# A one-hot product in four row strips, and a new order of the first splits

## What is computed

```
W   = weights[condition]                      # weights: 16 x 32 x 32, condition: 32 numbers in 0..15
mix = einsum('bct,bcd->bdt', x, W)            # every sequence b mixed by its own 32 x 32 matrix
q, k, v = mix @ Wq + bq, mix @ Wk + bk, mix @ Wv + bv        # 512 -> 4096, 32 heads of 128
```

## Time and profile before

| | us |
|---|---|
| median of 3 runs | 806.32 |
| lowest and highest of them | 806.26 and 807.01 |
| the profiled execution's own time | 805.49 |
| its span, first to last instruction | 803.7 |

### The profile page before, as it was taken

How to read it: one execution, slowest core, us unless ns; L and a number is a source line. 1 busy time by engine, 2 the same in 40 slices (tenths; PEclk the granted TensorE clock), 3 DMA queues, 4 the chain that set the end, 5 groups by cost and what they waited for, 6 DMA issues and landing times.

```text
span 803.7 us, 15196 instructions
## 1 busy us (share of the span) xinstructions
PE 795.6 (99%) x6093; PEld 651.7 (81%) x6093; DVE 643.1 (80%) x646; ACT 332.2 (41%) x374; POOL 520.5 (65%) x451
## 2 busy tenths in 40 slices
PE   9999999999999999999999999999999999999998
PEld 7777888888888888888888888888888888888466
DVE  7799888888888888987889769989899888861442
ACT  4655555555555555572222226322422331322520
POOL 4999887333333333428998995979999999910420
PEclk9999999999999999999999999999999999999999
DMA  7031111111111111304434421456404813418502
GB/s 207 28 85 50 52 52 52 53 52 52 52 52 52 52 52 42 115 2 157 182 139 180 180 105 55 169 79 187 157 1 157 316 61 147 157 50 257 127 18 88
DMA packets 80735, 81.87 MB, mean 102 GB/s; under 512 B 26044, under 2 KB 61212, under 8 KB 78652
## 3 DMA queue, kind: packets, MB, share of 16 engines
q1 hardware_dynamic: 80188, 81.24, 31.2%
q10 hardware_dynamic: 512, 0.13, 0.1%
HBM read 64.97 MB, written 16.40 MB: 101 GB/s over the span
## 4 chain that ended last, share of the span: by engine, by line
PE 91%; DVE 3%; POOL 3%; ACT 2%; DMA 1%; issue 1%; SPq 0%; DVEq 0%; POOLq 0%
PE psum L862 13%; PE psum L864 12%; PE psum L863 12%; PE psum L808 7%; PE psum L810 7%; PE psum L809 7%; PE psum L1061 7%; PE psum L1090 4%; PE psum L1092 4%; PE psum L1091 4%; PE psum L1078 3%; PE psum L1080 3%; PE psum L1079 3%; PE psum L901 3%; PE psum L1149 1%; DMA w_raw<-in_wk 1%
## 5 line engine op out<-in xcount | busy, mean ns | idle before, releaser
L506 POOL TENSOR_TENSOR w_raw<-w_raw 128x256 f32<-128x256 f32 x31 | 45.1, 1454 | 123.1 <-DMA w_raw<-in_wk 122.6
L862 PE MATMUL psum<-t_hi,w_hi 128*128 128x512 f32 x248 | 100.5, 405 | 0.0
L864 PE MATMUL psum<-t_hi,w_lo 128*128 128x512 f32 x248 | 96.5, 389 | 0.0
L863 PE MATMUL psum<-t_lo,w_hi 128*128 128x512 f32 x248 | 96.5, 389 | 0.0
L1370 ACT ACTIVATE sq<-qk_sb 128x1024 f32<-128x1024 f32 x31 | 32.9, 1063 | 140.7 <-issue 127.5
L1637 DVE TENSOR_TENSOR sumsq<-sumsq,sq 128x1024 f32<-128x1024 f32 x62 | 80.2, 1295 | 0.0
L1409 ACT ACTIVATE at_hi<-psum,params 128x512 fp32r<-128x512 f32 x64 | 44.0, 688 | 69.6 <-PE psum L1061 69.6
L862 PE MATMUL psum<-mix_hi,w_hi 128*128 128x512 f32 x186 | 72.5, 390 | 0.2 <-DVE w_lo L1541 0.2
L863 PE MATMUL psum<-mix_lo,w_hi 128*128 128x512 f32 x186 | 72.4, 389 | 0.0
L864 PE MATMUL psum<-mix_hi,w_lo 128*128 128x512 f32 x186 | 72.4, 389 | 0.0
L1541 DVE TENSOR_TENSOR w_lo<-w_raw,w_hi 128x1792 fp32r<-128x1792 f32 x30 | 61.4, 2047 | 1.5 <-ACT w_hi L1246 1.5
(11 more groups left out here) (287 smaller groups left out, 2130.2 us busy)
## 6 DMA issues: line engine op xcount, KB each, us to landing
v_sb<-v_scr_dram SPq DMA_DIRECT2D x6, 2048.0 KB, 7.9
v_scr_dram<-v_sb SPq DMA_DIRECT2D x9, 1024.0 KB, 3.9
w_raw<-in_wq SPq DMA_DIRECT2D x32, 256.0 KB, 2.9
w_raw<-in_wk SPq DMA_DIRECT2D x32, 256.0 KB, 3.2
wv_raw<-in_wv SPq DMA_DIRECT2D x16, 512.0 KB, 4.4
toep<-kpad_dram SPq DMA_DIRECT2D x2, 4096.0 KB, 14.5
wo_raw_a<-in_wo SPq DMA_DIRECT2D x4, 1024.0 KB, 5.2
wo_raw_b<-in_wo SPq DMA_DIRECT2D x4, 1024.0 KB, 5.2
```

The costliest lines, as they stand in the source:

```text
L862: mm(bank(n), wh, hi[:, c, tok], start=(i == 0), stop=False)
L863: mm(bank(n), wh, lo[:, c, tok], start=False, stop=False)
L864: last = mm(bank(n), wl, hi[:, c, tok], start=False, stop=(i == 1))
```

## The change

The product that chooses W is cut in four strips. `cond_nat` holds at partitions 0, 32, 64 and 96 the 16 rows of 256 numbers that belong to one quarter of the columns; two of these loads are issued by SyncE, two by ScalarE's queue behind `cond_i`, which now goes to all 128 partitions. Each strip is one matmul of 256 columns over 16 partitions at its own row position of the array, into a bank of its own (0 to 3). One semaphore count behind the last one replaces the two of before. The blanking of `cond_nat` goes; three small operations subtract 32, 64 and 96 from the partition numbers instead. Both turns into `mix_w` read all four banks. TensorE spins six times ahead of the product and eight times behind it. On ScalarE and VectorE the split of head 0's weights moves behind two groups, and VectorE writes the `mix_f` of group 4 one group later.

```diff
-            for n in range(2):
-                sp.dma_start(cond_nat[NCOND * n:NCOND * n + NCOND], cond_w.rearrange("n c d -> n (c d)")).then_inc(cond_in, 16)
+            for i in range(2):
+                sp.dma_start(cond_nat[32 * i:32 * i + NCOND], cond_cols[i]).then_inc(cond_in, 16)
...
-            spin(5, ones[:, :], 7)
-            pe.wait_ge(cond_in, 48)
+            spin(6, ones[:, :], 7)
+            pe.wait_ge(cond_in, 80)
             pe.wait_ge(hot_ok, 1)
-            pe.wait_ge(fill_ok, 2)
-            for n in range(2):
-                mm(bank(n), onehot[:].rearrange("n q b -> n (q b)"),
-                   cond_nat[:].rearrange("n (c d) -> n c d", d=32)[:, :, 16 * n:16 * n + 16],
-                   start=True, stop=True).then_inc(mixw_mm, 1)
-            spin(3, ones[:, :], 7)
+            for i in range(4):
+                rows = slice(32 * i, 32 * i + NCOND)
+                last = mm(bank(i, 256), onehot[rows].rearrange("n q b -> n (q b)"), cond_nat[rows, :],
+                          start=True, stop=True, tile_position=(32 * i, 0))
+            last.then_inc(mixw_mm, 1)
+            spin(8, ones[:, :], 7)
...
-            act.dma_start(cond_i[:], every_partition(cond_idx, BATCH, NCOND)).then_inc(cond_in, 16)
+            act.dma_start(cond_i[:], every_partition(cond_idx, BATCH)).then_inc(cond_in, 16)
+            for i in range(2, 4):
+                act.dma_start(cond_nat[32 * i:32 * i + NCOND], cond_cols[i]).then_inc(cond_in, 16)
...
+            for n in range(2):
+                mix_out(n)
             act.wait_ge(w_in[0], 32)
             sc.activation(w_hi[0][:, 0:4, :].rearrange("p b n -> p (b n)"),
                           w_raw[0][:, 0:4, :].rearrange("p b n -> p (b n)"), ACT.Copy).then_inc(whi0_ok, 1)
-            for n in range(G):
+            for n in range(2, G):
                 mix_out(n)
...
             v.memset(cond_f[:], -1.0).then_inc(zero_ok, 1)
-            v.memset(cond_nat[64:P], 0.0).then_inc(fill_ok, 1)
-            v.memset(cond_nat[32:64], 0.0).then_inc(fill_ok, 1)
+            dve.wait_ge(sel_const, 1)
+            for q in range(1, 4):
+                v.tensor_scalar(cond_no[quadrant(q)], cond_no[quadrant(q)], -32.0 * q, None, ALU.add).then_inc(row_ok, 1)
...
+            dve.wait_ge(mixw_mm, 1)
             for n in range(2):
-                dve.wait_ge(mixw_mm, n + 1)
-                v.transpose(mix_w[:].rearrange("p g (b d) -> p d (g b)", d=32)[:, 16 * n:16 * n + 16, :],
-                            bank(n).rearrange("p (c d) -> p d c", d=16)).then_inc(mixw_ok, 1)
+                rows = bank(0, 2048).rearrange("p (i w) -> p i w", i=4)[:, :, 0:256].rearrange("p i (c d) -> p d i c", d=32)
+                v.transpose(mix_w[:].rearrange("p g (b d) -> p d (g b)", d=32)[:, 16 * n:16 * n + 16, :].rearrange(
+                    "p d (i c) -> p d i c", i=4), rows[:, 16 * n:16 * n + 16]).then_inc(mixw_ok, 1)
...
+            mix_out(0)
+            mix_whole(0)
+            mix_out(1)
             dve.wait_ge(whi0_ok, 1)
             v.tensor_tensor(w_lo[0][:, 0:4, :].rearrange("p b n -> p (b n)"),
...
-            for n in range(G):
+            mix_out(2)
+            mix_whole(2)
+            for n in range(3, 6):
                 mix_out(n)
+            mix_whole(4)
+            mix_out(6)
+            mix_whole(6)
+            mix_out(7)
```

More of the change, by code:

```diff
@@ L135, in build_program @@
          (toep0,), (ax_hi, ax_lo), (scores,)) = overlay(
-            [("mix_w", [P, G, P], F32), ("cond_nat", [P, 32 * 32], F32),
-             ("cond_i", [NCOND, BATCH], I32), ("cond_f", [P, BPG, BATCH], F32), ("cond_no", [P, 1], F32),
+            [("mix_w", [P, G, P], F32), ("cond_nat", [P, 8 * 32], F32),
+             ("cond_i", [P, BATCH], I32), ("cond_f", [P, BPG, BATCH], F32), ("cond_no", [P, 1], F32),
              ("onehot", [P, BPG, BATCH], F32),
@@ L233, in build_program @@
         whi1_ok, wlo1_ok = sem("whi1_ok"), sem("wlo1_ok")
-        zero_ok, fill_ok, blank_ok = sem("zero_ok"), sem("fill_ok"), sem("blank_ok")
+        zero_ok, row_ok, blank_ok = sem("zero_ok"), sem("row_ok"), sem("blank_ok")
         prm_mm, prm_ok = sem("prm_mm"), sem("prm_ok")
@@ L282, in build_program @@
         out_rows = out.rearrange("(g p) f -> g p f", p=P)
+        cond_cols = [cond_w.rearrange("n c d -> n (c d)")[:, 256 * i:256 * i + 256] for i in range(4)]
         wqk_cols = [w.rearrange("(c p) n -> p c n", p=P) for w in (wq, wk)]
@@ L1525, in _ @@
             v.memset(cond_f[:], -1.0).then_inc(zero_ok, 1)
-            v.memset(cond_nat[64:P], 0.0).then_inc(fill_ok, 1)
-            v.memset(cond_nat[32:64], 0.0).then_inc(fill_ok, 1)
+            dve.wait_ge(sel_const, 1)
+            for q in range(1, 4):
+                v.tensor_scalar(cond_no[quadrant(q)], cond_no[quadrant(q)], -32.0 * q, None, ALU.add).then_inc(row_ok, 1)
             dve.wait_ge(zero_ok, 1)
-            dve.wait_ge(cond_in, 48)
-            own = cond_f[0:NCOND].rearrange("n q b -> n (q b)")
+            dve.wait_ge(cond_in, 80)
+            own = cond_f[:].rearrange("n q b -> n (q b)")
             own = bass.AP(own.tensor, own.offset, [list(own.ap[0]), [BATCH + 1, BPG], [BPG, G]])
@@ L1534, in _ @@
             dve.wait_ge(condf_ok, 1)
-            dve.wait_ge(sel_const, 1)
+            dve.wait_ge(row_ok, 3)
             v.tensor_scalar(onehot[:], cond_f[:], cond_no[:, 0:1], None, ALU.is_equal).then_inc(hot_ok, 1)
@@ L1564, in mix_out, with mix_whole @@
                 v.tensor_tensor(mix_lo[:, :, tok], src, mix_hi[:, :, tok].bitcast(F32), ALU.subtract).then_inc(mixlo_ok, 1)
-                if n not in MIXF_ACT:
-                    v.tensor_copy(mix_f[:, :, tok], src).then_inc(mixf_ok, 1)
+            def mix_whole(n):
+                tok = slice(P * MIX_ORDER[n], P * MIX_ORDER[n] + P)
+                v.tensor_copy(mix_f[:, :, tok], bank(2 + n % 6).rearrange("p (c t) -> p c t", c=KC)).then_inc(mixf_ok, 1)
+            mix_out(0)
+            mix_whole(0)
+            mix_out(1)
             dve.wait_ge(whi0_ok, 1)
```

## The result

| | before | after |
|---|---|---|
| median of the timed runs, us | 806.16 (18 runs, 805.47 to 809.35) | 808.03 (18 runs, 807.16 to 809.51) |
| profiled execution, own time, us | 805.49 | 807.46 |
| its span, us | 803.7 | 805.7 |
| start of head 2, us | 38.84 | 41.32 |

The ratio of after to before is 1.0023, with a 95% interval of 1.0017 to 1.003. The forecast was 806.2 with a range of 805.2 to 807.9: the kernel became slower, by 1.9 us, and stands just outside the range. Head 2, too, starts later than the 40 that the prediction had named as what would prove it wrong.

What follows compares the result with a forecast made beforehand. TensorE was taken as the bound, busy 795.6 of 803.7 us, so only an earlier start of head 2 could win. Its gain summed to 0.0; from 806.32, less a tenth for kinder loads, the forecast was 806.2, range 805.2 to 807.9.

Steps and rivals of the forecast that it cites:

- The loads: Start: the last `cond_nat` strip lands at 4.1, between 3.9 and 4.9, so the product starts at 4.8.
- it is issued a little ahead of the x rows: Reason given for a landing at 4.1, nearer to the 2.2 to 2.5 us of earlier `cond_nat` loads.
- The product: Eight float32 records of 256 columns overlap in four row strips: 1.1 us instead of 3.75, perhaps 0.3 longer.
- The third rival: Between product and first turn: row strips don't overlap, records take 3.4 us, run 808.3; chance 0.07.
- Turns and spins: Behind the product: `mix_w` ready at T + 3.4 = 8.2; eight spins run from 5.9 to 8.8 and set M.
- T: Start of the product on TensorE: 4.12 before, forecast 4.8 (4.6 to 5.6).
- TensorE's own filler takes most of what the strips give: Before the mixing: `mix_w` is ready 0.8 us earlier, but spins end at 8.8, against mixing at 9.02 before.
- M: Start of the mixing on TensorE: 9.02 before, forecast 8.8, the later of `mix_w` and the spins' end.
- The wait for the sixth `mix_lo`: Ahead of the first head: TensorE, ready at M + 8.02, waits 0.4 us until VectorE finishes at M + 8.4.
- The two engines slow each other in other places: VectorE and GpSimd slow each other; GpSimd was given 0.5 us to spare for that.
- The sum: Start of head 2 gains the smaller of 8.8 - M and 9.3 - M: 0.0 with M = 8.8.
- The early and late pace: Two rivals on when TensorE's pace doubles: earlier gives 805.7, chance 0.13; later gives 807.5, chance 0.17.

Runs made afterwards that it cites:

- run 6: Changed kernel with the numbers loaded to 16 partitions and the one-hot written four times, once per strip: 807.94 against 806.26 us, ratio 1.0028.
- run 7: run 6 with five spins behind the product instead of eight and `mix_f` of group 2 behind the sixth `mix_lo`: 807.66 us, ratio 1.0018.
- Run 5: Kernel before with one edit, the numbers loaded to all 128 partitions instead of 16: 807.26 against 806.26 us, ratio 1.0013.
- Run 12: Changed kernel with SyncE's first x loads held until the five small loads have landed, timed: 806.43 against 805.86 us, ratio 1.0004.
- run 3: Changed kernel with three spins behind the product instead of eight: 809.34 against 806.34 us, ratio 1.0044.
- Run 1: Kernel before with only the new order of the splits on ScalarE and VectorE: 807.28 against 806.34 us, ratio 1.001.
- run 2: Changed kernel with the splits back in the old order: 808.04 against 806.34 us, ratio 1.0014.
- run 4: Changed kernel with the number load last in ScalarE's queue instead of first: 810.71 against 806.34 us, ratio 1.0061.
- run 8: Changed kernel with SyncE's first x loads held until the five small loads have landed, one profiled execution: 806.11 us.
- run 10: Changed kernel with two strips of 512 columns, loaded by SyncE, numbers on 48 partitions, five spins, `mix_f` 2 and 4 late: 805.61 us, ratio 1.0.
- runs 9: Changed kernel with two strips of 512 columns, loaded by SyncE, numbers on 48 partitions, five spins, old split order: 806.24 us, ratio 1.0004.

## Why the prediction was wrong

*The loads: the step that failed.* "I take 4.1" for the landing of the last strip, with 4.9 as the worst. It was 5.88, and the product started at 6.65 where 4.8 was forecast. The upper bound was taken from the load that had the same place in the queue before, 3.2 us; but that row stood behind a number load in 16 pieces, and the change makes it 128. With the 16 pieces back, runs 6 and 7 land it in 3.0 and 2.9, within that bound. I had looked at the widening only for what computes on the numbers and given it no cost. Run 5 shows the omission alone (+1.66 us at the product, +1.0 us in the time). The other half, the x rows issued in the same moment, I had seen, and dismissed with "it is issued a little ahead of the x rows"; by the table above it is worth 1.1 to 2.0. Run 12 shows what the landing is worth: with the last strip at 4.17, near the 4.1 that I took, the time is 1.0004 times that of before. DMA in after, from a table of windows (us, then busy times, clock, DMA share, GB/s):

```profile
2.00:2.50 0.50, 0.50 (x5) 0.50 (x4) 0.00 (x0) 0.36 (x1) 0.50 (x1) 1.00 1.16 37
2.50:3.00 0.50, 0.50 (x4) 0.50 (x4) 0.00 (x0) 0.50 (x1) 0.33 (x1) 1.00 0.95 59
3.50:4.00 0.50, 0.42 (x2) 0.13 (x1) 0.00 (x0) 0.14 (x1) 0.00 (x0) 1.00 0.39 58
4.00:4.50 0.50, 0.00 (x0) 0.00 (x0) 0.00 (x0) 0.00 (x0) 0.00 (x0) 1.00 0.53 203
...
5.00:5.50 0.50, 0.00 (x0) 0.00 (x0) 0.00 (x0) 0.00 (x0) 0.00 (x0) 1.00 1.14 402
```

From 2.0 to 3.0 the DMA share is 1.16 and 0.95 at 37 and 59 GB/s; after that it falls to about a half while the strip is still not there, and the transfers reach 402 GB/s only at 5.0. Before, the rate was higher already from 2.0 on:

```profile
2.00:2.50 0.50, 0.50 (x5) 0.50 (x4) 0.23 (x2) 0.49 (x2) 0.50 (x1) 1.00 0.51 148
...
3.50:4.00 0.50, 0.00 (x0) 0.00 (x0) 0.46 (x2) 0.00 (x0) 0.35 (x2) 1.00 1.04 376
```

In run 6, with 16 pieces and the x rows in the same place, it was

```profile
2.00:2.50 0.50, 0.50 (x5) 0.50 (x4) 0.00 (x0) 0.36 (x1) 0.50 (x1) 1.00 0.42 74
```

So the wide load goes with a low rate and a late landing. How it delays its neighbours is not shown: in run 5, where it costs 1.7 us, the share from 2.0 to 2.5 is only 0.40, and in the trace of after the 128 small pieces themselves take 0.01 us each, spread from 1.8 to 3.5. That the engines are simply full of them does not fit.

*The product.* 1.17 us, predicted 1.1: the strips go through the array together, in float32 too. The third rival, strips in series, is dead, and its 808.3 was near the measured time for another reason. Against eight records in series at the slow pace, 8 x 0.43 = 3.4, the strips go 2.9 at a time; that is nearer to the 3.07 of the Trainium skill, "TensorE: Matmul & The Clock Gate", section "Measured speedup vs the span model" (measured there with 32 rows and 512 columns), than to four. Put the other way: 0.3 us stand above the 0.86 of four strips at a time. The prediction had 0.24 of them as switch and weight load and, by the page, 0.3 more for a smaller overlap, 1.4 in all, which was not measured; which of the two the 0.3 are is not shown.

*Turns and spins.* The turns end at T + 3.3 (3.4 predicted) and the spins take 3.08 us, all but the last five records at 0.21 or more. The mixing starts 0.95 us behind `mix_w`, so "TensorE's own filler takes most of what the strips give" was right, with more filler than I thought. M is 10.90 where 8.8 was forecast; all but 0.25 of that comes with T. But the spins' time is not free to be had: runs 3 and 7 begin the mixing 1.5 and 1.2 us sooner than after (0.6 and 0.4 of it by an earlier product), and head 2 stands where it stood, at 41.35 in both. The "earlier product" of run 3 is the scatter of the landing.

*The wait for the sixth `mix_lo`.* 0.4 predicted, 1.00 measured. The order and the counts in it were right; the term I mis-sized is `w_lo`, taken at the 1.22 that it had when GpSimd was idle. Beside GpSimd's sums it takes 1.80, which is 0.58 of the 0.6 us missing. "The two engines slow each other in other places" stood in the text, as a remark on GpSimd's slack and not in TensorE's sum. Run 1 shows this wait without the strips.

*The sum.* By the prediction's formula head 2 moves by 8.8 - M = -2.1, and the longer wait takes 0.6 more: -2.7, to 41.5; it stands at 41.32. The formula held, its inputs did not. The two terms, each alone on the kernel before, cost 0.9 (run 1) and 1.0 us (run 5) in the timed runs, by their intervals 0.1 to 1.5 and 0.3 to 1.7; together they match the 1.9 of after, which leaves for the strips' own gain about nothing. That last is a difference of three medians and is not shown closer than a microsecond.

*The early and late pace.* Both rivals are real, as mechanisms: the doubling came about 8.1 in the profile of before, 10.4 in after, 13.7 in run 2, and by 5.0 and at 9.6 in two executions of one kernel. In the profile of after the mixing ran fast from its first record, so the pace took nothing there; its spins split much as the prediction had them, and the loss is not the late pace. It sits in the scatter between executions, 2.35 us from the fastest to the slowest timed run of after, and whether the later product makes the late pace more frequent stays open.

## What to carry to other kernels

At the start of a kernel, price a small load by how many pieces the loads ahead of it and beside it have, not by its own bytes, and put what TensorE waits for ahead of the bulk loads in time, whatever the queue. When an operation is moved, take its duration from a row in which its new neighbour is running: two-input work of VectorE put beside GpSimd's sums costs both. And a gain on an engine that fills its idle time with spins must be followed through the filler before it is counted.

## What the runs showed of the hardware

- A load of one row of 128 bytes to 128 partitions, 16 KB in all, takes 1.6 to 2.2 us when it is first, and 6.1 when it is issued third, beside 512 KB loads (run 4). Ahead of others it makes them 0.6 to 1.7 us later (the table, and run 5).
- Float32 matmuls in four row strips of 16 rows and 256 columns overlap: eight records in 1.17 us at the slow pace, 0.64 at the fast (run 8), against 3.4 in series.
- The granted clock reads 1.00 in every half microsecond from 1 to 20 us, in all the profiles, while 128-column records are 0.21 us apart at first and 0.11 later, the spacings of 1.2 and 2.4 GHz. The change between them came anywhere from about 4.3 (run 10) to 15.2 us (run 4) after the start, and some 4.6 us apart in two executions of one kernel. In runs 9 and 10 TensorE worked without a wait from 0.99 through the product, and it came at 10.6 in the one and at 4.3 in the other.
- VectorE's comparison took 0.30 us on 16 partitions as on 128.
- VectorE's `w_lo`, with two operands in SBUF, took 1.22 us alone and 1.80 when it began 0.01 to 0.02 us behind a sum of GpSimd, whose next sum then took 1.59 instead of 0.73 (runs 1 and 2, after).
